# One weight product for values and output, a gate in column tiles, halved experts and a new instruction order in a one-core fusion block

## What is computed

```python
feat = conv2x2_stride2(x, conv_w) + conv_b            # (16, 144, 64): 4 channels x 36 tokens
Q, K, V = feat @ wq.T + bq, feat @ wk.T + bk, feat @ wv.T + bv
h = (softmax(Q @ K.T / 8) @ V) @ wo.T + bo
h = concat([h, txt], axis=1)                          # (16, 272, 64)

a = layernorm(h)                                      # mixer
pos     = scan of (a @ Wvp + bvp) with cos and sin of base_phases
kp, qp  = tanh(tanh(a @ Wk1 + bk1) @ Wk2 + bk2) * pi, and the same with the q weights
content = causal sum over t of cos(qp_s - kp_t) * (a @ Wvc + bvc)_t, scaled
gates   = softmax(relu(a @ Wg1 + bg1) @ Wg2 + bg2)    # two gates
h = h + a + (layernorm(gates[0]*pos + gates[1]*content) * ln_g + ln_b) @ Wo + bo

f = layernorm(h)                                      # 8 experts, two best of each token
w = softmax over the two largest of (f @ Wg + bg), zero elsewhere
h = h + sum over e of w[e] * (gelu(f @ W1[e] + b1[e]) @ W2[e] + b2[e])
```

## Time and profile before

| | |
|---|---|
| median of 3 runs | 257.95 us |
| the three runs | 256.1, 257.95, 263.72 us |
| profiled execution, span from its first to its last instruction | 254.6 us |
| busy in the span: PE, PEld, DVE | 232.3, 128.0, 170.6 us |
| busy in the span: ACT, POOL | 158.7, 100.7 us |
| chain of work that ended last | PE 61%, DVE 21%, ACT 9%, issue 6% |
| mean granted TensorE clock | 0.991 |

### The profile page before, as it was taken

How to read it: one execution, slowest core, us unless ns; L and a number is a source line. 1 busy time by engine, 2 the same in 40 slices (tenths; PEclk the granted TensorE clock), 3 DMA queues, 4 the chain that set the end, 5 groups by cost and what they waited for, 6 DMA issues and landing times.

```text
span 254.6 us, 4573 instructions
## 1 busy us (share of the span) xinstructions
PE 232.3 (91%) x1511; PEld 128.0 (50%) x1511; DVE 170.6 (67%) x526; ACT 158.7 (62%) x295; POOL 100.7 (40%) x88
## 2 busy tenths in 40 slices
PE   7879788878778899999999989999999999999993
PEld 5667565656456547645644334335333533344551
DVE  0987979999999979897558526574862753326223
ACT  2579997776593768595397443664366465474650
POOL 2000436774636431337166452360535131434132
PEclk9999999999999979999999999999999999999999
DMA  7650000000000000063000860001950009500522
GB/s 224 172 225 4 1 3 0 0 3 0 3 3 0 3 0 3 5 173 76 0 0 9 190 140 4 0 0 23 236 111 0 0 28 239 113 0 3 161 48 62
DMA packets 12902, 14.41 MB, mean 57 GB/s; under 512 B 6448, under 2 KB 10576, under 8 KB 12752
## 3 DMA queue, kind: packets, MB, share of 16 engines
q1 hardware_dynamic: 12304, 13.66, 21.2%
q10 hardware_dynamic: 576, 0.47, 0.6%
HBM read 12.87 MB, written 1.25 MB: 55 GB/s over the span
## 4 chain that ended last, share of the span: by engine, by line
PE 61%; DVE 21%; ACT 9%; issue 6%; DMA 1%; POOLq 0%; POOL 0%; DVEq 0%; ACTq 0%
PE ps L1070 24%; PE ps L1083 23%; ACT probs L504 3%; DVE trig L756 2%; DVE stat L637 2%; DVE feat L618 2%; DVE y L746 2%; PE ps L993 2%; PE ps L1030 2%; PE ps L1004 1%; DMA arena<-in_x_a 1%; DVE mem L766 1%; PE ps L1038 1%; DVE negmax L695 1%; PE ps L933 1%
## 5 line engine op out<-in xcount | busy, mean ns | idle before, releaser
L592 ACT ACTIVATE arena<-ps,cols 128x1024 f32<-128x1024 f32 (+2 forms) x80 | 74.0, 984 | 45.9 <-PE ps L1070 34.2
L1070 PE MATMUL ps<-xt,w 64*128 64x512 f32 (+2 forms) x320 | 69.2, 556 | 1.0 <-ACT arena L592 0.4
L1083 PE MATMUL ps<-arena,w 128*64 128x512 f32 (+2 forms) x320 | 64.9, 538 | 0.7 <-ACT arena L592 0.7
L463 POOL TENSOR_TENSOR acc<-acc,scaled 128x512 f32<-128x512 f32 (+2 forms) x35 | 39.6, 1131 | 63.9 <-DVE scaled L841 63.0
L428 POOL TENSOR_TENSOR rstd<-vare,minus_half 128x8 f32<-128x8 f32 (+2 forms) x15 | 25.6, 1710 | 65.0 <-DVE vare L646 65.0
L1070 PEld LDWEIGHTS ps<-xt,w 64*128 64x128 f32 x320 | 29.1, 189 | 32.4 <-issue 23.9
L841 DVE SCALAR_TENSOR_TENSOR scaled<-ps,b_col,wide 128x512 f32<-128x512 f32 (+2 forms) x35 | 23.3, 667 | 31.1 <-PE ps L1083 26.7
L1083 PEld LDWEIGHTS ps<-arena,w 128*64 128x64 f32 x320 | 20.5, 136 | 38.1 <-issue 26.4
L451 POOL TENSOR_TENSOR cum<-cum,turn_n 128x544 f32<-128x544 f32 x8 | 12.1, 1517 | 15.5 <-DVE cum L750 15.5
L504 ACT ACTIVATE probs<-ps,negmax 72x144 f32<-72x144 f32 x32 | 11.6, 375 | 1.3 <-DVE negmax L695 1.3
L618 DVE SCALAR_TENSOR_TENSOR feat<-arena,cols,feat 128x144 f32<-128x144 f32 x24 | 7.1, 362 | 6.6 <-ACT feat L478 6.5
(11 more groups left out here) (136 smaller groups left out, 385.1 us busy)
## 6 DMA issues: line engine op xcount, KB each, us to landing
wide<-rows_of SPq DMA_DIRECT2D x24, 256.0 KB, 5.9
wide<-rows_of SPq DMA_DIRECT2D x8, 192.0 KB, 4.0
w<-in_w SPq DMA_DIRECT2D x1, 1024.0 KB, 5.0
wide<-rows_of SPq DMA_DIRECT2D x8, 128.0 KB, 3.2
out<-res SPq DMA_DIRECT2D x6, 128.0 KB, 2.6
h0s<-in_txt SPq DMA_DIRECT2D x1, 512.0 KB, 6.6
w<-in_w SPq DMA_DIRECT2D x1, 512.0 KB, 5.8
arena<-in_x_a SPq DMA_DIRECT2D x1, 288.0 KB, 3.7
```

The costliest lines, as they stand in the source:

```text
L463: pool.tensor_tensor(acc[:, g % 2, 0:128 * GW[g]], acc[:, g % 2, 0:128 * GW[g]], scaled[:, i % 2, 0:128 * GW[g]], ALU.add).then_inc(S["acc ...
L592: act.activation(hidden_e[:, k % 4, 0:2 * n].rearrange("p (h t) -> p h t", h=2), ps[:, bank("expert", i, j):bank("expert", i, j) + 2, 0:n] ...
L1070: ins = pe.matmul(ps[:, bank("expert", i, j) + h, 0:n], w1[r, c:c + 128], xt[r, GC[g]:GC[g] + n], start=True, stop=True)
L1083: ins = pe.matmul(ps[64 * h:64 * h + 64, bank("expert_out", i), 0:n], w2[:, 2 * (i % E) + j, :], hidden_e[:, (2 * i + j) % 4, n * h:n * h ...
```

## The change

1. `wv` and `wo` are multiplied once, at the start (a transpose, one 128-column product and one bias product on PE, three copies on ACT: `fold_t`, `fold`). `qkv` multiplies by the product, `mix` writes h directly with one bias, `tok_out` and its copy are gone.
2. The gate: `mix_gate` holds the 32 weight columns and streams the windows, each into 32 PSUM rows of its own; ACT does bias and positive part (`gate_h`), PE one small product (`gate_z`), ACT the tanh from PSUM. DVE prepares its weights once (`gate_w`, seven operations).
3. `moments` takes five small operations; the factors 1/2 and 8 move into the two wide operations.
4. Groups 3, 4, 4, 3, 3; eight Gelu buffers, shared with the early tiles; the unit of PLAN for the first expert product and Gelu is a half.
5. The convolution runs in three sets of pairs (2, 3, 3), each loaded by its own DMAs; `base` stands first on DVE, ACT and POOL; ACT issues `ident`, `cols`, a table load, `rows`, `phase`.
6. Seven warm-up products in place of ten: five first, one after the transpose, one after the products of item 1.
7. PLAN and BANKS are new.

```diff
-GW = [3, 4, 4, 4, 2]
+GW = [3, 4, 4, 3, 3]
-WARM_UP = 10
+WARM_UP = [5, 1, 1]
+PAIR_SETS = [(0, 2), (2, 5), (5, 8)]
+HIDDEN = 8
...
+            act.dma_start(ident[:, :], const_d[:, 0:128]).then_inc(ld["ident"], 16)
+            act.dma_start(cols[:, :], cols_d).then_inc(ld["cols"], 16)
+            act.preload_act_table(ACT.Exp)
+            act.dma_start(rows[:, :], rows_d).then_inc(ld["rows"], 16)
             act.dma_start(phase[:, :, :], phase_d).then_inc(ld["phase"], 16)
...
-                    act.activation(mixed[:, i % 2, :], ps[:, bank("mix", i), 0:SI], ACT.Identity, bias=col("bv"))\
-                elif stage == "tok_out":
-                    act.wait_ge(S["tok_mm"], i + 1)
+                    act.activation(h0s[:, i, 0:SI], ps[:, bank("mix", i), 0:SI], ACT.Identity, bias=bvo[:, :])\
...
+                    if i >= HIDDEN:
+                        act.wait_ge(S["e2_mm"], (i - HIDDEN) // 2 + 1)
...
-                dve.tensor_tensor(msum[:, 0:n], st[:, :, 1], st[:, :, 4], ALU.add)
-                dve.tensor_tensor(mvar[:, 0:n], st[:, :, 2], st[:, :, 5], ALU.add)
+                dve.tensor_tensor(total, st[:, :, 1], st[:, :, 4], ALU.add)
+                dve.scalar_tensor_tensor(out=mvar[:, 0:n], in0=st[:, :, 2], scalar=64 * EPS, in1=st[:, :, 5],
+                                         op0=ALU.add, op1=ALU.add)
                 link(dve.tensor_tensor(mdif[:, 0:n], st[:, :, 1], st[:, :, 4], ALU.subtract))
-                dve.tensor_scalar(mean[:, kind, g % 2, 0:n], msum[:, 0:n], 0.5, None, ALU.mult)
...
+            warm_up(WARM_UP[0])
+            pe.wait_ge(ld["tokw"], 16)
+            pe.wait_ge(ld["ident"], 16)
+            pe.transpose(ps[:, FOLD_BANK, 0:128], wv, ident[:, :]).then_inc(S["fold_t"], 1)
+            warm_up(WARM_UP[1])
+            pe.wait_ge(S["wv_t"], 1)
+            pe.wait_ge(ld["cols"], 16)
+            pe.matmul(ps[:, FOLD_BANK, 128:256], wv_t[:, :], wo, start=True, stop=True)
+            pe.matmul(ps[:, FOLD_BANK, 256:257], wo, col("bv"), start=True, stop=True).then_inc(S["fold"], 1)
+            warm_up(WARM_UP[2])
...
-                        ins = pe.matmul(ps[:, bank("mix_gate", i), 32 * w:32 * w + 32], xt[:, c:c + 128], diag(g1_w),
+                        ins = pe.matmul(ps[32 * w:32 * w + 32, bank("mix_gate", i), 0:128], diag(g1_w), xt[:, c:c + 128],
...
 PLAN = {
...
-qkv:0 qkv:1 exps:0 exps:1 probs_t:0 qkv:2 qkv:3 probs_t:1 exps:2 exps:3 mix:0 mix:1 qkv:4 tok_out:0 tok_out:1
+base:0 tap0:0 tap0:1 tap0:2 fold_t:0 fold:0 qkv:0 qkv:1 exps:0 qkv:2 exps:1 qkv:3 probs_t:0 exps:2 mix:0 qkv:4
```

433 lines of the change are left out of this document (234 added, 199 removed), and 4 rows, old and new, of the table BANKS.

## The result

The changed kernel is slower: 269.28 us median (267.06 to 270.7, four runs) against 260.26 us of the kernel before in the same series (256.1 to 263.72), a ratio of 1.043 with a 95% interval from 1.034 to 1.053. The forecast was 254.0, range 246 to 263. The profiled execution took 270.7 us with a span of 268.8. A ratio compares only the executions that lie within 1.5% of the fastest of their kernel, so it can differ from that of the medians, and the profiled executions of after_filled and old_order_filled lie above this limit.

The account below looks back on a forecast made before the run. DVE and ACT were taken to bound the front (to the first expert product), PE the back; 254.6 + 7.5 - 11.3 + 0.8 = 251.6 profiled, 254.0 forecast between shifts from median (254.95) and fastest (253.1), range 246 to 263.

Parts of the forecast that it names:

- The start: Up to the first exponential: base ahead of the first tap puts it at 22.7 us, 8.8 later.
- From the first exponential to the first expert product: Middle stretch: 70.5 us against 71.8 before, between bounds of 75.9 by ACT and 64.5 by DVE.
- The clock rival: Early part: PE stays at the lower clock level, 0.63 us lost per us, about 272 us at worst; chance 0.13.
- The back: First expert product to first product of the last finish: 11.3 us shorter, bounds 6 and 15.
- 7.4 + 3.1: PE work in the back: 7.4 us less by mixer stages moved, 3.1 less by fewer runs of expert products.
- The 0.8 for waits and clock: In the back: 1.5 us saved at the lower clock, less 0.7 for new waits behind the first experts.
- third rival: In the back: longer expert runs save nothing, waits at 39 turns eat about 6 us, 260 us; chance 0.13.
- The tail: Last sums and last store, on three windows instead of two: 0.8 us longer than 5.2.
- first rival: The front is not later: first expert product at about 88 us, time 247 us; chance 0.20.
- Dear table loads: Extra table loads on ACT cost 13.5 us instead of 6.4, time 261 us; chance 0.02.

Follow-up runs that it names:

- after_filled: Changed kernel with 16 warm-up products behind the transpose and 25 products of ones where PE waits; 272.5 us, ratio 1.040 to 1.063.
- old_order_filled: New operations in the order, groups, image sets and banks of the kernel before, plus eight unused products of ones on PE; 267.93 us.
- warm_start: Changed kernel with 16 warm-up products in place of one behind the transpose; 266.24 us, ratio 1.003 to 1.062.
- reordered: Changed kernel with 16 warm-up products behind the transpose, normalisation of groups 2 and 3 ahead of streams, and middle reordered on PE, ACT, DVE; 263.4 us.
- warm_norms: Changed kernel with 16 warm-up products behind the transpose and normalisation of groups 2 and 3 ahead of streams on DVE; 266.1 us, ratio 1.018 to 1.035.
- expert_early: Changed kernel with 16 warm-up products behind the transpose and mixer work of pairs 6 and 7 behind the first three expert halves; 280.43 us.
- old_gate_filled: Order of the kernel before with folded weight, five-op layer norm, eight Gelu buffers, half experts, old gate, plus eight unused products on PE; 253.96 us.
- base_late: Changed kernel with base put back behind the fourth normalisation (DVE) and fourth transposed probabilities (ACT); 269.37 us, ratio 1.040 to 1.051.
- norms_first: Changed kernel with normalisation of groups 2 and 3 ahead of the streams of pairs 1 and 2 on DVE; 266.95 us, ratio 1.026 to 1.048.
- fewer_loads: Changed kernel with sines grouped so that five table loads, not nine, stand between the exponentials and Gelu's load; 269.5 us, ratio 1.023 to 1.060.

## Why the prediction was right and wrong

*The start* (predicted first tap 11.5, first exponential 22.7; measured 9.57 and 21.92) was right within 1 us at its end, with errors inside. `phase` landed at 5.92 (6.5 taken). The load issued between the DMAs held none of them back: the issues behind it stand at 1.66 and 2.19, so 0 was right. `base` on ACT took 1.2 us and not 2.6, because its table load ran at 2.92, while ACT waited. These rows of ACT's timeline answer to the earlier trace rows:

```profile
1.63 1.28 ACT L508 ACT_TABLE_LOAD   x1 [1.63 <-PEq L1227]
1.66 0.50 ACTq L509 DMA_DIRECT2D rows<-in_rows  x1
2.19 0.46 ACTq L510 DMA_DIRECT2D phase<-in_phase  x1
2.92 1.28 ACT L531 ACT_TABLE_LOAD   x1
8.36 0.43 ACT L531 ACTIVATE turn_p<-phase 128x272 f32<-128x272 f32 x1 [4.16 <-DVE phase L730]
...
9.57 4.38 ACT L519 ACTIVATE arena<-arena,cols 128x72 f32<-128x72 f32 x12
```

Against these gains stood the lower clock, at which the projections ran: warm_start took 2.4 off. The prediction had put that into a rival, not into this term.

*From the first exponential to the first expert product* (70.5; measured 86.1) is the step that failed. I bounded the stretch by ACT (75.9) and DVE (64.5) and left PE out, as "seldom the last", and I took the mixer work moved ahead of the first expert as work for which "PE has room". DVE's busy time is 64.6, so that engine's sum was good, but no engine's sum set the stretch, which at the full clock (80.6) lies over both. PE became the largest part of the chain that ended last: 37.4 us of it, against 5.3 before, and 23.2 still in warm_start with the clock nearly full. PE's idle time there was waiting in a chain through three engines, and it did not shrink when work was put in: in warm_start it was 16.95 us (12.97 before) beside 2.9 us more of PE work. By the runs the miss of 15.6 divides into some 5 for the clock (warm_start: 0.2 for each of 27 us) and some 10 for moved work and waits at the full clock. Of these reordered avoids about 2.6, some 1.5 of it by the edits of warm_norms. How the rest splits between work and waits was not settled: expert_early, made for it, brought waits of its own. The sizes fit moved work that was not hidden at all: at the full clock the stretch is 80.6, or 8.8 longer than before, beside the 7.4 us of PE work that the prediction reckoned to move out of the back (net of what left the stretch, the products of `tok_out` among it, 2.9 by warm_start). In old_gate_filled, with most of the new operations in the old order, it takes 69.9, about what I forecast, and the back 163.7, as before. Set against these, the new order has a back 8.7 shorter and a stretch 10.7 longer at the full clock: it moved time from the back to the front and gained nothing by it.

*The clock rival* (0.13) had the right mechanism and the wrong place and price. It looked at 15 to 45 us and reckoned 0.63 us lost per us. The lower level stood at 10 to 20 as it said, but the larger part came behind waits at 40 to 105 us. One us at it costs 0.2 us by warm_start, as PE is only part of the chain. Of the 27 us in the stretch it thus makes 5, which alone would have made some 259 of the 254. That its 272 lies near the measured 269.28 is luck.

*The back* (152.4, wrong "if it is not 150 to 155"; measured 154.98) came out just inside, and its work was right. PE's busy time fell by 161.18 - 149.17 = 12.0 us; some 1.7 of this is the clock (3.4 us at the lower level before, none now), and the other 10.3 stand against 7.4 + 3.1 = 10.5. The 0.8 for waits and clock had the wrong sign: the clock gave its 1.7, but PE's idle time rose from 2.6 to 5.8, 3.2 more, with the longest wait at the transposes of combine:

```profile
176.75 0.55 PE L1084 MATMUL ps<-ident,comb 128*128 128x128 f32 x3 [1.50 <-DVE comb L710]
```

So the third rival (runs that save nothing) fell: the work went down as reckoned, and new waits of 3.2 ate less than a third of it. In warm_start, base_late, norms_first and fewer_loads, which keep it, the back lasted 155.0 as well.

*The tail* (6.0) took 5.8. Of the first rival (front not later) nothing was seen. Dear table loads: each load of the changed kernel took 1.28, as before.
